# A two-layer attention and expert kernel: its first half's norms turned by DMA transposes, and the seam in another order

## The reference, cut to what matters

```python
xn = _layernorm(ctx, gamma_media, beta_media)             # c: the context
ln = _layernorm(_layernorm(x), gamma_lat, beta_lat)       # x: the rows, normed twice
q = ln @ Wq + bq
kv = concatenate([xn, ln], axis=1) @ Wkv + bkv
attn = softmax(q * DH ** -0.5 @ k.T)                      # 8 heads, 256 x 512 each
x = x + (attn @ v) @ Wo + bo
```

## Time and profile before

| | |
|---|---|
| median of 3 runs | 1827.29 us (1826.53 to 1829.1) |
| the profiled execution's own time | 1824.9 us |
| its span in the trace | 1823.0 us |
| busy in the span | PE 98%, DVE 81%, ACT 73%, POOL 30% |
| mean granted TensorE clock | 0.998 of full speed |
| one batch in the middle of the first half | about 57 us |

### The profile page before, as it was taken

One profiled execution on the slowest core, in us unless ns is written; L12 is line 12 of the kernel. 1 busy time (PEld: TensorE's weight loads), 2 busy tenths in 40 slices (PEclk: granted clock), 3 DMA queues, 4 the chain that ended last, 5 costly groups with the idle time before them and its releaser, 6 DMA issues.

```text
span 1823.0 us, 40134 instructions
## 1 busy us (share of the span) xinstructions
PE 1785.5 (98%) x12818; PEld 1658.1 (91%) x12818; DVE 1468.9 (81%) x3544; ACT 1328.9 (73%) x2554; POOL 543.6 (30%) x714
## 2 busy tenths in 40 slices
PE   7999999999999999999899999999999999999999
PEld 5888888888888888888788999999999999999998
DVE  7888888888888787787567888888888888888876
ACT  5878778887778777777576677777767777776753
POOL 3354434544344533445543111111111111111100
PEclk9999999999999999999999999999999999999999
DMA  5565555545554444444619644343443434344300
GB/s 153 106 134 135 113 138 143 139 117 127 135 132 99 87 92 86 98 98 88 137 41 292 159 73 95 65 89 72 88 88 72 95 66 90 70 87 88 72 7 13
DMA packets 370652, 185.92 MB, mean 102 GB/s; under 512 B 307744, under 2 KB 355744, under 8 KB 370592
## 3 DMA queue, kind: packets, MB, share of 16 engines
q1 hardware_dynamic: 361888, 150.55, 34.5%
q0 software_dynamic: 8704, 34.61, 10.6%
HBM read 97.29 MB, written 21.23 MB: 65 GB/s over the span
## 4 chain that ended last, share of the span: by engine, by line
PE 82%; DVE 8%; issue 3%; ACT 3%; DMA 2%; POOL 1%; SPq 0%; DVEq 0%; POOLq 0%; ACTq 0%
PE ring L741 9%; PE ring L743 9%; PE ring L742 9%; PE ring L2083 8%; PE ring L2085 8%; PE ring L2084 8%; PE sim L2085 3%; PE sim L2083 3%; PE sim L2084 3%; PE sim L741 3%; PE sim L742 2%; PE sim L743 2%; PE ps_x L741 2%; PE ps_x L742 2%; PE ps_x L743 2%
## 5 line engine op out<-in xcount | busy, mean ns | idle before, releaser
L411 POOL TENSOR_SCALAR a_parts<-a_pr,a_rinv 128x512 f16<-128x512 f32 x240 | 174.5, 739 | 470.6 <-DVE a_rinv L656 411.5
L2083 PE MATMUL ring<-b_xch,b_wel 128*128 128x256 f32 x1024 | 288.6, 282 | 0.5 <-DVE b_act_e L1696 0.5
L2085 PE MATMUL ring<-b_xcl,b_weh 128*128 128x256 f32 x1024 | 286.4, 280 | 0.0
L2084 PE MATMUL ring<-b_xch,b_weh 128*128 128x256 f32 x1024 | 286.1, 279 | 0.0
L2084 PEld LDWEIGHTS ring<-b_xch,b_weh 128*128 128x128 f32 x1024 | 193.4, 189 | 0.0
L2083 PEld LDWEIGHTS ring<-b_xch,b_wel 128*128 128x128 f32 x1024 | 192.1, 188 | 0.7 <-DVE b_act_e L1696 0.7
L2085 PEld LDWEIGHTS ring<-b_xcl,b_weh 128*128 128x128 f32 x1024 | 192.1, 188 | 0.0
L504 ACT ACTIVATE a_pr<-sim,a_nmax 128x512 f32<-128x512 f32 x256 | 173.7, 688 | 21.1 <-DVE a_nmax L645 20.7
L1404 ACT ACTIVATE b_heh<-b_act_e 128x512 fp32r<-128x512 f32 x128 | 80.7, 631 | 135.8 <-DVE b_act_e L1696 114.4
L665 DVE SCALAR_TENSOR_TENSOR a_parts<-a_pr,a_rinv,a_parts 128x512 f16<-128x512 f32 x240 | 179.1, 786 | 0.0
L645 DVE TENSOR_REDUCE a_nmax<-sim 128x1 f32<-128x512 f32 x256 | 164.8, 680 | 10.1 <-PE sim L743 10.1
(11 more groups left out here) (369 smaller groups left out, 6474.3 us busy)
## 6 DMA issues: line engine op xcount, KB each, us to landing
b_w2l_raw<-in_W2T POOLq DMA_DIRECT2D x16, 1088.0 KB, 8.8
b_even_b<-rows_between SPq DMA_DIRECT2D x16, 1024.0 KB, 5.5
b_w1l_raw<-in_W1T POOLq DMA_DIRECT2D x16, 1024.0 KB, 8.4
b_w1l_raw<-in_We SPq DMA_DIRECT2D x8, 768.0 KB, 4.6
expert_halves<-b_w1h SPq DMA_DIRECT2D x8, 768.0 KB, 3.4
expert_halves<-b_w1l SPq DMA_DIRECT2D x8, 768.0 KB, 4.8
b_weh<-expert_halves SPq DMA_DIRECT2D x8, 768.0 KB, 8.7
b_wel<-expert_halves SPq DMA_DIRECT2D x8, 768.0 KB, 10.1
```

What stands on the lines that cost most here:

```text
L411: nc.gpsimd.tensor_scalar(parts[:, 0, t, :], pr[:, h % 2, t, :], rinv[:, h % 2, t:t + 1], 1.0, ALU.mult, ALU.mult).then_inc(prob_ready, 1)
L2083: nc.tensor.matmul(out, ll, rh, start=(n == 0), stop=False)
L2084: nc.tensor.matmul(out, lh, rh, start=False, stop=False)
L2085: last = nc.tensor.matmul(out, lh, rl, start=False, stop=(n == len(parts) - 1))
```

## The change

For batches 1 to 15 the norms no longer go through PE. POOL writes a high f16 plane of each normed tile (`ln_high`: context in slot 0, rows in slot 3), DVE the low one (`ln_low`: end of slot 2, and slot 4 behind the low half of Q3), and SP turns the four planes with DMA transposes (`ln_cross`). ACT applies gamma and beta to the high plane (`affine_high`: end of slot 3 and end of slot 5), and DVE adds the low plane and splits (`joined_halves`: in slot 5 ahead of K7's low half, and in slot 5 behind O4's). Batch 0 is turned by PE as before. The buffers lie where the second half's w2 planes come later, so the clearing of these planes' padding moves from batch 0 to the seam.

```diff
+        def ln_cross(b, k):
+            take(kv_ready, b * 2 - 1 + k)
+            for part in range(2):
+                take(ln_part, (b - 1) * 4 + 2 * k + part + 1)
+                sp.dma_start_transpose(ln_turned[:, k, part].rearrange("p t c q -> p (t c) q"),
+                                       ln_parts[:, k, part].rearrange("p t d -> p (t d)")).then_inc(lnT_ready, 16)
...
                 if nxt and h + 1 < H:
                     cross(b, h + 1)
+                if nxt and h < 3:
+                    ln_cross(b + 1, h - 1)
...
+        def ln_high(b, k):
+            take(ln_ready, b * 3 + 2 * k + 1)
+            if k == 1:
+                take(ln_part, (b - 1) * 4 + 2)
+            nc.gpsimd.tensor_scalar(ln_parts[:, k, 0], (c_ln, x_ln2)[k][:], LN_SCALE, 1.0, ALU.mult, ALU.mult)\
+                .then_inc(ln_part, 1)
...
+                    if h == 0:
+                        ln_high(b + 1, 0)
+                if nxt and h == 3:
+                    ln_high(b + 1, 1)
...
+        def affine_high(b, k):
+            g, bb = ((gms, bm), (gls, bl))[k]
+            act.wait_ge(lnT_ready, (b - 1) * 64 + 2 + 32 * k + 32)
...
-                    if j == 1 and h == H - 4 and nxt:
-                        affine(b + 1, 0)
-                    if j == 2 and h == H - 4 and nxt:
-                        affine(b + 1, 1)
+                    if j == n - 1 and h == 3 and nxt:
+                        affine_high(b + 1, 0)
+                    if j == n - 1 and h == H - 3 and nxt:
+                        affine_high(b + 1, 1)
...
+        def ln_low(b, k):
+            dve.wait_ge(ln_part, (b - 1) * 4 + 2 * k + 1)
+            nc.vector.scalar_tensor_tensor(ln_parts[:, k, 1], (c_ln, x_ln2)[k][:], LN_SCALE, ln_parts[:, k, 0],
+                                           ALU.mult, ALU.subtract).then_inc(ln_part, 1)
+        def joined_halves(b, k):
+            done = (b - 1) * 4 + 2 + 2 * k
+            dve.wait_ge(aff_ready, b * 2 + k + 1)
+            for c in range(DC):
+                last = nc.vector.scalar_tensor_tensor(
+                    aff[:, k, c, :].rearrange("p (t q) -> p t q", t=ST), ln_turned[:, k, 1, :, c, :], (gms, gls)[k][:, c:c + 1],
+                    aff[:, k, c, :].rearrange("p (t q) -> p t q", t=ST), ALU.mult, ALU.add)
...
-                    kv_halves(b + 1, 0)
+                    joined_halves(b + 1, 0)
...
-                    if j == 0 and h == H - 3 and nxt:
-                        kv_halves(b + 1, 1)
+                    if j == 1 and h == H - 3 and nxt:
+                        joined_halves(b + 1, 1)
...
+                    if j == n - 1 and h == 2 and nxt:
+                        ln_low(b + 1, 0)
+                    if j == 1 and h == 4 and nxt:
+                        ln_low(b + 1, 1)
...
-                    if j == 0 and h == H - 4 and nxt:
-                        if prev:
-                            pe.wait_ge(x1_ready, b)
-                        transposes(b + 1)
```

```diff
@@ scalar
-            if (h, done) == (0, ("K", 2)):
+            if (h, done) == (0, ("O", 7)):
                 weight_high(0, "1", 0)
                 weight_high(0, "1", 1)
...
                 copy_high(0, "A", xth[:])
-                for q in range(4):
-                    weight_high(0, "2", q)
...
             if (h, done) == (1, ("O", 0)):
                 gelu_high(0, 1)
+                weight_high(0, "2", 0)
+                weight_high(0, "2", 1)
@@ vector
-            if h == 7:
-                rows_apply(1)
-        def beside(h, done):
-            if (h, done) == (0, "begin"):
+        def beside(h, done):
+            if (h, done) == (0, "maxima"):
+                rows_apply(1)
                 dve.sem_inc(acc_ready, 2)
                 dve.wait_ge(x1_in, 16)
                 norm_stats(0, "A", x1_s)
@@ tensor
-                for t in range(ST):
-                    project_out(b, order, i + 1, t)
-                    other.beside(H, ("W", t))
+                project_out(b, order, i + 1, 0, range(H - 1))
+                project_out(b, order, i + 1, 1, range(H - 1))
+                project_out(b, order, i + 1, 0, range(H - 1, H))
+                other.beside(H, ("W", 0))
+                project_out(b, order, i + 1, 1, range(H - 1, H))
+                other.beside(H, ("W", 1))
```

More of the change, by code:

```diff
@@ L78, in crossing, with ln_crossing @@
         return Region(low.nc, (low.top + 127) // 128 * 128 + 2 * 8 * KB + 64, 8 * KB)
+    def ln_crossing(self):
+        low = self.of["low"]
+        return Region(low.nc, (low.top + 127) // 128 * 128 + 2 * 8 * KB + 64 + 8704, 8704)
 @dataclass
@@ L221, in latent_attention @@
     crossing = mem.crossing()
+    ln_crossing = mem.ln_crossing()
+    ln_parts, ln_turned = ln_crossing.put("a_ln_parts", [P, 2, 2, ST, D], F16), ln_crossing.put(
+        "a_ln_turned", [P, 2, 2, ST, DC, P], F16)
+    gms, gls = ln_crossing.put("a_gms", [P, DC]), ln_crossing.put("a_gls", [P, DC])
     parts, turned = crossing.put("a_parts", [P, 2, ST, SK], F16), crossing.put("a_turned", [P, 2, ST, KT, P], F16)
@@ L397, in norm_apply @@
             if k != 1:
-                take(lnT_ready, b * 2 - 1 + k // 2)
+                take(lnT_ready, (b - 1) * 64 + 2)
             for t in range(ST):
@@ L460, in affine @@
                                             bias=bb[:, c:c + 1], scale=g[:, c:c + 1])
+            last.then_inc(aff_ready, 1)
+        def affine_high(b, k):
+            g, bb = ((gms, bm), (gls, bl))[k]
+            act.wait_ge(lnT_ready, (b - 1) * 64 + 2 + 32 * k + 32)
+            for c in range(DC):
+                last = nc.scalar.activation(aff[:, k, c, :].rearrange("p (t q) -> p t q", t=ST), ln_turned[:, k, 0, :, c, :],
+                                            ACT.Identity, bias=bb[:, c:c + 1], scale=g[:, c:c + 1])
             last.then_inc(aff_ready, 1)
@@ L474, in scalar @@
         act.wait_ge(c_small, 16 * 2)
+        nc.scalar.activation(gms[:], gm[:], ACT.Copy, scale=1.0 / LN_SCALE)
+        nc.scalar.activation(gls[:], gl[:], ACT.Copy, scale=1.0 / LN_SCALE)
         nc.scalar.activation(bq_s[:], bq_raw[:], ACT.Copy, scale=QSCALE).then_inc(bq_ready, 1)
@@ L592, in kv_halves @@
             dve.wait_ge(kv_hi, b * 2 + k + 1)
+            nc.vector.tensor_tensor(kvl[:, :, k * S:(k + 1) * S], aff[:, k], f32(kvh[:, :, k * S:(k + 1) * S]),
+                                    ALU.subtract).then_inc(kv_ready, 1)
+        def ln_low(b, k):
[5 more added lines that the diff above has]
+            dve.wait_ge(aff_ready, b * 2 + k + 1)
+            for c in range(DC):
+                last = nc.vector.scalar_tensor_tensor(
+                    aff[:, k, c, :].rearrange("p (t q) -> p t q", t=ST), ln_turned[:, k, 1, :, c, :], (gms, gls)[k][:, c:c + 1],
+                    aff[:, k, c, :].rearrange("p (t q) -> p t q", t=ST), ALU.mult, ALU.add)
+            last.then_inc(kv_hi, 1)
+            dve.wait_ge(kv_hi, done + 1)
+            nc.vector.tensor_copy(kvh[:, :, k * S:(k + 1) * S], aff[:, k]).then_inc(kv_hi, 1)
+            dve.wait_ge(kv_hi, done + 2)
             nc.vector.tensor_tensor(kvl[:, :, k * S:(k + 1) * S], aff[:, k], f32(kvh[:, :, k * S:(k + 1) * S]),
@@ L822, in project_out @@
                 last.then_inc(wo_full, 1)
-        pe.wait_ge(consts, 1)
+        pe.wait_ge(pool_step, 3)
         transposes(0)
@@ L864, in turn @@
                         pe.wait_ge(w_lo, split("O0"))
-                    pe.wait_ge(aff_ready, b * 2 + 4)
+                    if prev:
+                        pe.wait_ge(x1_ready, b)
                     for t in range(ST):
@@ L1267, in early @@
                 for e in range(E):
-                    nc.gpsimd.memset(index[:, e:e + 1], float(e))
-                for c in range(HC):
-                    last = nc.gpsimd.memset(f32(w2_raw[:, c * W2ROW + D:(c + 1) * W2ROW]), 0.0)
+                    last = nc.gpsimd.memset(index[:, e:e + 1], float(e))
                 last.then_inc(consts, 1)
@@ L1284, in ahead @@
                 update(0, "1", 3)
+            if h == 7:
                 weights_added(0, "1")
-            if h == 7:
                 rows_rstd(1)
@@ L1290, in beside @@
             if (h, done) == (0, "begin"):
+                pool.wait_ge(first.sems["kv_ready"], 2 * B)
+                for c in range(HC):
+                    nc.gpsimd.memset(f32(w2_raw[:, c * W2ROW + D:(c + 1) * W2ROW]), 0.0)
+                update(0, "2", 0)
                 rstd_of(0, "A")
-                update(0, "2", 0)
                 update(0, "2", 1)
@@ L1478, in ahead @@
                 rows_in_order(0)
-            if h == 7:
+        def beside(h, done):
+            if (h, done) == (0, "exps"):
                 rows_in_order(1)
-        def beside(h, done):
-            if (h, done) == (0, ("K", 2)):
+            if (h, done) == (0, ("O", 7)):
                 weight_high(0, "1", 0)
                 weight_high(0, "1", 1)
-            if (h, done) == (0, ("Q", 1)):
+            if (h, done) == (0, ("V", 4)):
```

18 lines of the change are left out of this document (10 added, 8 removed).

## The result

| | before | after |
|---|---|---|
| median | 1827.7 us (1826.53 to 1829.1, 4 runs) | 1928.37 us (1927.12 to 1929.15, 4 runs) |
| ratio | 1 | 1.055, 95% interval 1.0535 to 1.0565 |
| profiled execution | 1824.9 us | 1927.95 us |
| mean granted TensorE clock | 0.998 | 0.973 |

A forecast was written before the change was run, and what follows sets the result against it. PE, busy 98% of the span, was taken as the bound. 1824.9 + 67.5 (turns) + 12 (clock) - 10 (seam) = 1894.4 us profiled, given as a 1896 us median; range 1855 to 1925 us.

The forecast's parts named there:

- O4 to K0, clock included: From O4's start to K0 in each turn: 0.3 us of added lateness, plus the falling clock's share.
- 15 turns: Turns 0 to 14: 67.5 us of lateness plus 12 us for the clock falling in a third of them.
- seam: Between the halves: W2's reordered high halves and DVE's reordered batch 15 start shorten PE's waits, -10 us (-4 to -12).
- Off PE: Eight transposes leave PE's path, 0.79 us in each of 15 turns, 11.9 us; the saving is used up inside.
- SP's queue: Slots 3 and 4: SP waits for the rows' low plane, delaying head 4's transposes; O4 4.2 us late (3.2 to 4.8).
- After O4: DVE's low part of head 5, joined halves and low halves before K0: 0.3 us more a turn (0 to 0.8).
- The clock: Gaps ahead of O4 drop PE's clock in a third of the turns, five times 2.5 us: +12 (0 to 37).
- rival A: The clock falls in every turn, 15 x 2.5 = 37 in place of 12: 1922 us; chance 0.14.
- The range: For the whole kernel's time: 1855 to 1925 us, taking in rival A and B's upper part.
- B: Rival: SP's hold is mostly covered, 2.0 us a turn are left, 1847 us; chance 0.14.
- C: Rival: everything new is hidden, head 4's low transpose issued by 464.2; faster, 1805 us; chance 0.07.
- DVE's 3 us more a batch fit in its 9.4 us of idle time: Later slots: DVE's added work fits its idle time in each batch and is costed at nothing.

The follow-up runs named there:

- the fillers: The changed kernel with 20 idle identity products issued by TensorE ahead of its wait for head 4's cast in every turn: 1908.41 us.
- all the mends: Changed kernel, second norm's transposes behind head 4's pair, low planes by GpSimd, its residual-and-bias sum in slot 6, second norm's joined halves sooner: 1819.28 us.
- the first experiment: The changed kernel with SyncE's two transposes of the second norm put behind head 4's pair instead of ahead of it: 1841.29 us, 1.0079 of before.
- 1829: The kernel of the first experiment with VectorE's second-norm joined halves one place sooner in slot 5, ahead of the inverses and O4's low half: 1828.92 us.

## Why the prediction was wrong, and where it was right

The direction, the place and the mechanism were right: SyncE's queue, the low plane in slot 4, O4, K0. Two sizes were off by 0.9 us a turn each, 13.5 us over 15 turns: how late O4 comes, and what the clock takes behind it. Together they put the result 3 us above the range; either of the two alone would have left it inside.

| term | forecast | measured |
|---|---|---|
| O4 late | 4.2 us a turn (3.2 to 4.8) | 5.1 |
| O4 to K0, clock included | 0.3 + 0.8 | 2.0 |
| 15 turns | +79.5 | about +111, by subtraction of the seam; the two rows above give 107 |
| seam | -10 | -10.2 to -10.4 |

- *Off PE.* The transposes' 0.8 us are gone from the row; scores(5) and (6) start 0.6 and 0.4 us later behind what stands in front of them. That this saving would be used up inside was right.
- *SP's queue.* This step was mis-sized by 0.9 us. Q3's low half came 0.8 us later against the batch's start than before, the upper end and not near the middle: VectorE's low planes of head 4 began 0.9 us later, and took 2.44 us where they took 1.91. From there to O4 the chain had 8.1 us where I had added up 7.8: SyncE took 1.55 us from the plane's transpose to head 4's high one (1.35 assumed), 3.2 from the low one's issue to its cast (3.1), and 1.2 from the cast's start to O4 (1.1). The "ends" of this term covered only when Q3 comes, and gave the chain behind it no slack.
- *After O4.* The 0.3 us were right in kind: with the clock held up by the fillers K0 comes 6.2 us after O4 (turns 2 to 14), before the change 5.7, so it is 0.5.
- *The clock* is the step that failed. I took the one fall of the seam, 4.0 us after the last matmul, as the length that a gap must have, and so gave the falls a third of the turns. They came in all 15, from 2.4 us into the gap on. This was rival A, at a chance of 0.14. Its price of 2.5 us was too high: 1.3 net by the fillers. Fifteen times 1.3 is 20, against 12.
- *The range* was drawn narrower than its own terms: the ends 84 (turns), 37 (clock) and -10 add up to 1938 us with the 1827.3 of before. Rival A, at 1922, was priced with the middle lateness only. The sum itself comes to 1894.4 + 2.4 = 1896.8; that it is given as 1896 changes nothing.
- *The seam* was right, and adds to the rest.
- *B and C.* B did not hold: nothing of SyncE's hold was covered. C's point of decision, an issue by 464.2 or 17.9 us after the batch's start, was well placed. Before, head 4's low transpose stood at 463.24 - 446.29 = 16.95; with all the mends it goes out after 17.61, with the order alone mended after 18.32, and in both the wait ahead of O4 is gone (PE's own row did not reach O4 0.79 us sooner, as C had taken, so there was a little more room). What then decides is VectorE's row: 1841, 1829 and 1819 us by how much of it is cleared. The 1805 us of C, the whole worth of the transposes, was reached by none.
- *"DVE's 3 us more a batch fit in its 9.4 us of idle time"* was wrong as well, though hidden at first. The added work lies in slots 2 to 5, where VectorE follows PE with hardly a gap. In the first experiment's batch 7 it has no idle stretch above 0.2 us from 459.1 to 492, and then 1.40 us in slot 6 and several of 0.4 to 1.0 up to the next batch's slot 0. The first experiment's turns show what it costs: 58.5 to 58.8 us after 57.6 in batches 1 to 8, 58.4 to 58.8 after 56.9 in 9 to 13, the transposes' saving already in them.

## What to carry to other kernels

A queue that serves transfers in order is an engine like any other: each transfer put into it must be priced as the wait for its source plus its place (here 6.0 us together, the place at most 2.3), and put behind the one that PE needs next. Idle time of an engine helps an added operation only in the slot where it lies; look at the engine's row between the last two waits of PE, not at its share of the batch. And where a forecast stall is a few microseconds long, one observed gap does not say how long a gap the clock survives: give the falling clock its own large chance.
